# Query projections and one MLP projection of a cross-attention kernel: seven block products in place of eight

## The reference

```python
qh = (q_in @ wq + bq).reshape(b, q_len, H, K)      # H = 16 heads, K = 128
kh = (kv_in @ wk + bk).reshape(b, t, H, K)
vh = (kv_in @ wv + bv).reshape(b, t, H, K)
...
logits = jnp.einsum('bqhk,bthk->bhqt', qh, kh) / scale
weights = jax.nn.softmax(logits, axis=-1)
ctx = jnp.einsum('bhqt,bthk->bqhk', weights, vh).reshape(b, q_len, H * K)
return ctx @ wo + bo
...
h = jax.nn.gelu(h @ w_fc1 + b_fc1, approximate=False) @ w_fc2 + b_fc2   # 512 -> 2048 -> 512
```

## Time and profile before

| | us |
|---|---|
| median of 3 runs (lowest, highest) | 2988.18 (2986.56, 2992.95) |
| the profiled execution, its own time | 2985.3 |
| span in its profile | 2983.5 |
| mean granted TensorE clock | 0.978 of full speed |

### The profile page before, as it was taken

How to read it: one execution, slowest core, us unless ns; L and a number is a source line. 1 busy time by engine, 2 the same in 40 slices (tenths; PEclk the granted TensorE clock), 3 DMA queues, 4 the chain that set the end, 5 groups by cost and what they waited for, 6 DMA issues and landing times.

```text
span 2983.5 us, 40485 instructions
## 1 busy us (share of the span) xinstructions
PE 2823.4 (95%) x14352; PEld 2118.4 (71%) x14352; DVE 1902.5 (64%) x2743; ACT 1099.0 (37%) x2409; POOL 535.6 (18%) x373
## 2 busy tenths in 40 slices
PE   5989898997989999999999999999999999999899
PEld 2333333333778888888888878788888888888687
DVE  5989989897866555556555474565555655555644
ACT  3232323322534333334333343343343433433432
POOL 2857657473001000000000010010000000000100
PEclk8999899998999999999999999999999999999999
DMA  4010010111143222222222211132222222222111
GB/s 164 1 30 29 16 42 0 58 43 43 61 155 124 82 72 94 80 92 82 82 87 77 96 67 63 43 113 81 98 81 82 84 75 98 81 84 75 53 49 56
DMA packets 140224, 215.64 MB, mean 72 GB/s; under 512 B 10033, under 2 KB 76593, under 8 KB 139025
## 3 DMA queue, kind: packets, MB, share of 16 engines
q1 hardware_dynamic: 137264, 210.70, 20.3%
q0 software_dynamic: 2880, 3.94, 0.7%
HBM read 164.53 MB, written 46.14 MB: 71 GB/s over the span
## 4 chain that ended last, share of the span: by engine, by line
PE 64%; DVE 4%; DMA 1%; ACT 1%; issue 1%; DVEq 0%; ACTq 0%; SPq 0%
PE ca_ps L60 19%; PE ca_ps L62 19%; PE ca_ps L61 19%; PE ca_ps L1991 4%; PE ca_ps L1981 4%; DVE ca_stats L68 1%; DMA xres<-pb_dram 1%; PE ca_ps L2018 1%; DVE ca_pb L1745 1%; DMA pb_dram<-ca_pb 0%; ACT ca_pr L1552 0%; DVE ca_pr L1741 0%; DVE ca_mx L1733 0%; DVE ca_ctx_lo L1786 0%; DVE raw L1755 0%
## 5 line engine op out<-in xcount | busy, mean ns | idle before, releaser
L1552 ACT ACTIVATE ca_pr<-ca_ps,ca_nb 128x129 f32<-128x129 f32 x512 | 181.8, 368 | 487.8 <-DVE ca_nb L1735 487.7
L60 PE MATMUL ca_ps<-ca_h_hi,ca_wq_hi 128*128 128x512 f32 x768 | 313.2, 408 | 4.4 <-DVE ca_h_lo L1780 3.9
L617 DVE TENSOR_TENSOR_SCAN tm_xn<-tm_wd,tm_vb 128x512 f32<-128x512 f32 x256 | 298.5, 1208 | 12.7
L1505 POOL TENSOR_TENSOR ca_dv<-ca_bvr 128x256 f32<-128x256 f32 x32 | 23.6, 739 | 1563.7 <-DVE xq L1720 1404.5
L62 PE MATMUL ca_ps<-ca_h_hi,ca_wq_lo 128*128 128x512 f32 x768 | 302.8, 394 | 0.0
L61 PE MATMUL ca_ps<-ca_h_lo,ca_wq_hi 128*128 128x512 f32 x768 | 301.6, 393 | 0.0
L60 PE MATMUL ca_ps<-ca_wv_hi,ca_ctx_hi 128*128 128x256 f32 x1024 | 296.2, 289 | 2.1 <-DVE ca_wv_lo L1715 2.1
L62 PE MATMUL ca_ps<-ca_wv_hi,ca_ctx_lo 128*128 128x256 f32 x1024 | 286.7, 280 | 0.0
L61 PE MATMUL ca_ps<-ca_wv_lo,ca_ctx_hi 128*128 128x256 f32 x1024 | 286.6, 280 | 0.0
L60 PE MATMUL ca_ps<-ca_wo_hi,ca_ct_hi 128*128 128x512 f32 x640 | 256.0, 400 | 1.0 <-DVE ca_ct_lo L1749 0.8
L61 PE MATMUL ca_ps<-ca_wo_lo,ca_ct_hi 128*128 128x512 f32 x640 | 252.7, 395 | 0.0
(11 more groups left out here) (232 smaller groups left out, 5966.5 us busy)
## 6 DMA issues: line engine op xcount, KB each, us to landing
pb_dram<-ca_pb SPq DMA_DIRECT2D x128, 256.0 KB, 2.0
xres<-pb_dram SPq DMA_DIRECT2D x128, 256.0 KB, 2.7
ca_sq<-in_wq SPq DMA_DIRECT2D x49, 512.0 KB, 5.9
ca_so<-in_wo SPq DMA_DIRECT2D x48, 512.0 KB, 3.8
ca_sk<-in_wk SPq DMA_DIRECT2D x33, 512.0 KB, 6.9
ca_sv<-in_wv SPq DMA_DIRECT2D x32, 512.0 KB, 4.0
x_dram<-xres SPq DMA_DIRECT2D x8, 1024.0 KB, 4.2
ca_bvr<-in_bvb SPq DMA_DIRECT2D x32, 256.0 KB, 5.3
```

Of the source, the lines that this page charges most:

```text
L60: pe.matmul(out, lhs[0], rhs[0], start=first, stop=False)
L617: v.tensor_tensor_scan(state[t % 2][:, d, :], wd[:, g].rearrange("p b t -> p (b t)"), pair[:, d, :], 0.0, ALU.mult, ALU.add).then_inc(scan ...
L1552: ins = act.activation(pr[hd][:, b, :], ps[:, BANK_SC + b // 2, o:o + KW], ACT.Exp, bias=nbs[hd][:, b:b + 1], scale=SCALE, accum_out=sms[h ...
```

## The change

In all slots of the attention stages (the first two units of a stage stay as they are) and in the 14 `mlp_slot`s of the second half, the two query projections of a unit (24 matmuls of 512 columns) become `fast`: the product of a 512 x 256 weight block with 512 rows is cut into 2 x 2 blocks and made by Strassen's seven block products, each 2 chunks x 3 matmuls of 256 columns, so 42 matmuls of 256 columns. The products 1 and 6 share bank 0 and the products 2 and 7 share bank 2 (bank 1 in the MLP).

Sums of weight blocks (four for each pair of heads) and of row blocks (four for each quad and stage) are made by POOL, with their `hi` parts by ACT and `lo` parts by DVE (those of the rows by POOL). DVE combines the seven products into the four quarters of the two queries. Sums are also written in place over parts of `wq` and `h` that the plain units have finished with. To make room, `pr` and `pb` (probabilities and transposed blocks) have one buffer in place of two, the output bias is loaded for one stage at a time, and the context of the second half is loaded later (its buffer holds row sums of the first half). Several semaphores are merged. The last pair of a stage is taken out of the loop.

```diff
@@ tensor block @@
+            def fast(C, banks):
+                pe.wait_ge(wq_split, C.wq * 2 + 2)
+                pe.wait_ge(ws_split, C.ws * 2 + 2)
+                pe.wait_ge(t_split, (C.stage * 2 + C.quad) * 3 + 3)
...
+                product(out[0], a11, b11).then_inc(fast_full, 1)
+                product(out[1], s2, t2).then_inc(fast_full, 1)
+                product(out[2], s3, t3).then_inc(fast_full, 1)
+                product(out[3], s1, t1).then_inc(fast_full, 1)
+                product(out[4], a12, b21).then_inc(fast_full, 1)
+                pe.wait_ge(p1_read, C.fast + 1)
+                product(out[0], a22, minus_t4).then_inc(fast_full, 1)
+                pe.wait_ge(fast_sum, C.sums + 1)
+                product(out[1], s4, b22).then_inc(fast_full, 1)
...
             def scores(A, hd):
-                pe.wait_ge(q_out, A.n * 2 + (hd + 1))
+                pe.wait_ge(q_out, A.n * 2 + 2)
...
             def slot(A, C):
                 scores(A, 0)
-                query(C, 0, BANK_Q)
                 key(C, 0)
                 scores(A, 1)
-                query(C, 1, BANK_Q)
+                pe.wait_ge(o_out, A.o * 4)
+                fast(C, Q_BANKS)
                 key(C, 1)
-                value(C, 0, A.o * 4 - 1)
+                pe.wait_ge(q_out, C.n * 2 + 2)
+                value(C, 0, A.o * 4)
                 context(A, 0)
...
             def mlp_slot(B, M, C):
-                for k in range(2):
-                    pe.wait_ge(gelu_ready, M.m * 2 + (k - 3))
-                    hidden(M, k)
+                if M.h == 1:
+                    pe.wait_ge(gelu_step, M.m * 4 - 1)
+                    fast(M, M_BANKS)
...
                 mlp_out(B)
@@ vector block @@
             def slot(A, C):
                 row_max(A, 0)
                 normalise(A, 0)
+                key_col(C, 0)
                 row_max(A, 1)
+                fast_last_quarter(C)
+                normalise(A, 1)
                 if C.quad == 0:
-                    key_col(C, 0)
                     split_one(wv, sv, wv_hi, wv_split, C.wkv)
                 else:
                     split_one(wo, so, wo_hi, wo_split, C.wq)
-                normalise(A, 1)
+                fast_other_quarters(C)
                 if C.quad == 1:
                     split_q(C.wq + 1, 0)
-                else:
-                    key_col(C, 1)
-                if C.quad == 1:
-                    split_q(C.wq + 1, 1)
+                    if more_sums(C):
+                        split_q_fast(C.wq + 1)
+                    else:
+                        split_q(C.wq + 1, 1)
+                key_col(C, 1)
+                if C.quad == 1 and more_sums(C):
+                    weight_sums_lo(N)
+                    weight_sum_in_place_lo(N)
+                value_out(C, 0)
                 context_lo(A, 0)
-                value_out(C, 0)
...
+            def mlp_slot_fast(B, M):
+                if M.quad == 1:
+                    split_one(wo, so, wo_hi, wo_split, M.wq)
+                hidden_quarters(M)
...
+                add_output(B, 0)
+                gelu_lo(M, 0)
+                gelu_lo(M, 1)
+                add_output(B, 1)
+                add_output(B, 2)
+                if M.quad == 1 and more_sums(M):
+                    weight_sums_lo(N)
+                    weight_sum_in_place_lo(N)
+                add_output(B, 3)
@@ scalar block @@
             def second(A, C):
...
                 query_out(C, 1, BANK_K)
-                split_q(C.wq + 1, 1)
+                split_q_fast(C.wq + 1)
+                weight_sum_in_place_hi(N)
+                row_in_place_hi(C)
@@ gpsimd block, after the first pair of a stage @@
+                for g in range(1, G):
+                    if g < G - 1:
+                        gp.wait_ge(fast_full, 7 * unit(g, 1).fast + 7)
+                        weight_sums(unit(g + 1, 0))
+                        weight_sum_in_place()
+                    if g < len(biases):
+                        value_bias(biases[g])
```

More of the change, by code:

```diff
@@ L1294, in cross_attend @@
     TB = 32
+    HALF = QT // 2
+    Q_BANKS, M_BANKS = (0, 2, 3, 4, 7), (0, 1, 5, 4, 7)
     LN_BANKS = (0, 1, 5, 6)
@@ L1372, in __init__ @@
                 self.ln = (h * 3 + st) * 2 + quad
+                self.stage = h * 2 + st
+                self.fast = g * 2 + (quad - 2 + 14 * self.stage)
+                self.sums = self.fast * 5
+                self.plain = 4 * self.stage + 2 * quad + 32 * h
+                self.ws = g + (7 * self.stage - 1)
         class MlpUnit:
@@ L1384, in __init__, with more_sums, sums_before @@
                 self.u = cT if quad else uT
+                self.stage = 4
+                self.fast = g * 2 + (quad - 2 + 14 * self.stage)
+                self.sums = self.fast * 7 - 112
+                self.plain = self.m * 2 + (8 + 8 * h)
+                self.ws = g + (7 * self.stage - 1)
         def units(engine, h, st, slot):
-            with engine.Fori(1, G) as g:
+            with engine.Fori(1, G - 1) as g:
                 slot(Unit(h, st, g - 1, 1), Unit(h, st, g, 0))
                 slot(Unit(h, st, g, 0), Unit(h, st, g, 1))
+            slot(Unit(h, st, G - 2, 1), Unit(h, st, G - 1, 0))
+            slot(Unit(h, st, G - 1, 0), Unit(h, st, G - 1, 1))
+        def more_sums(C):
+            return not isinstance(C.g, int)
+        def sums_before(ln):
+            return 4 * (ln if ln < 4 else max(4, ln - 2))
         def mlp_units(engine, h, slot):
@@ L1462, in _ @@
                     more = h == 0 or i < 15
-                    if h == 0 and i == 1:
-                        for quad in range(2):
-                            sp.wait_ge(c_split, quad + 1)
-                            ctx_in(1, quad)
+                    if i % 8 == 1:
+                        next_bo(h, i // 8)
                     if i > 0:
@@ L1474, in _ @@
                     sp.wait_ge(wq_split, (q + 1) * 2)
+                    sums_taken(h, i)
                     sp.dma_start(sq[:], io["wq"][i + 1]).then_inc(wq_in, 16)
@@ L1480, in _ @@
                     sp.dma_start(so[:], io["wo"][i + 1]).then_inc(wo_in, 16)
+                    if h == 0 and i == 15:
+                        sp.wait_ge(fast_full, 7 * 28)
+                        for quad in range(2):
+                            ctx_in(1, quad)
                 probs(h, 15, 1)
@@ L1486, in _ @@
                     q = h * 24 + i
+                    if i == 17 and h == 0:
+                        next_bo(h, 2)
                     if h == 0 and i == 18:
@@ L1527, in _ @@
+            value_bias(0)
+            stage(0, 0, range(1, 9))
+            stage(0, 1, range(9, 17))
+            add_bo(0, 2, 0)
+            add_bo(0, 2, 1)
+            stage(1, 0, range(17, 25))
+            stage(1, 1, range(25, 32))
+            stage(1, 2, ())
         @block.scalar
@@ new lines, in quarter, with fast_last_quarter @@
+            def quarter(C, hd, out, bank, u):
+                return v.scalar_tensor_tensor(out=out, in0=ps[:, bank, 0:HALF], scalar=head_col(C, "bq", hd), in1=u, op0=ALU.add, op1=ALU.add)
+            def fast_last_quarter(C):
+                v.wait_ge(q_out, C.n * 2)
+                fast_u(C, qT[0][:, 0:HALF], Q_BANKS)
+                quarter(C, 1, qT[1][:, HALF:QT], Q_BANKS[3], u3[:]).then_inc(fast_sum, 1)
+                v.tensor_tensor(x1[:], x1[:], ps[:, Q_BANKS[3], 0:HALF], ALU.add).then_inc(fast_sum, 1)
```

353 lines of the change are left out of this document (290 added, 63 removed).

## The result

The changed kernel takes **3082.04 us** (median of 4 runs, 3071.42 to 3087.90) against 2987.55 of the kernel before: a ratio of 1.031, 95% interval 1.028 to 1.034. The forecast was 3016 within 2980 to 3046: the right sign, and three times too small. The profiled execution took 3071.42 (span 3069.6 against 2983.5).

What follows compares the result with a forecast made beforehand. PE, busy 95% of the span, was taken as the bound. The terms 0 + 7 + 3 + 8 + 3.5 + 4 + 4 = 29.5 on the profiled 2985.3 gave 3014.8; forecast 3016 us, range 2980 to 3046.

Steps and rivals of the forecast that it cites:

- PE's 0.70: Attention slots: PE alone gains about 0.70 us each from the seven products, from 12.89 to 12.19 before the value matmuls.
- PE stays the bound: Rival: DVE's line behind product 4 is shorter by 0.7 or more, each attention slot gains 0.70, 2976 us; chance 0.13.
- near zero: Rival: DVE's line is shorter by about 0.5 a slot, giving 2988 us; chance 0.07.
- 0 for 56 slots: Attention slots: PE's gain becomes an equal wait for DVE's second query, so slots do not get shorter; +-0.3 a slot.
- +7 us: 24 attention slots of quad 1: POOL's weight sums hold DVE's `lo` part, 0.3 a meeting; bounds 0 and 26.
- Weight loads set the pace: Rival: `fast` cannot hide its 42 weight loads, so attention and MLP slots get longer, 3180 us; chance 0.02.
- Joints between steps: Stage joints: scores wait for both queries, +3 at four passing steps; late exponentials, +8 at four first slots.
- Row sums of a stage lie in POOL's idle time: Five stages: row sums fit POOL's idle time but meet DVE's `lo` parts in `second`, +3 us.
- In the MLP's first `fast` ... +3.5: MLP's first `fast`: PE waits for weight sums that can only start after the last plain projection, +3.5 us.
- MLP slots +4: Seven pairs of MLP slots: block 3 waits for DVE's addition of block 1, +4 us; bounds -7 and +12.

Runs made afterwards that it cites:

- run 6: Changed kernel with the splits of the value and output weights moved to the head of the slot on ACT and DVE: 3035.41 us.
- run 11: run 9 with its new one-element tile allocated last, so that the other tiles lie as in run 8: 2975.12 us, ratio 0.9966 to the kernel before.
- run 8: Changed kernel with a plain last MLP, the slots of run 6 and the joints' work rearranged on POOL, DVE, ACT and PE: 2983.87 us.
- run 7: Changed kernel with DVE adding the MLP's second output block ahead of the `lo` part of the second Gelu: 3068.44 us.
- run 1: Changed kernel with the plain `mlp_slot` and its sums put back for half 1, attention left as changed: 3044.93 us.
- run 3: Changed kernel with ACT reading the passing step's two queries ahead of the `hi` parts of weight and row sums: 3088.71 us.
- run 4: Changed kernel with the first quad's row sums split earlier, their `hi` parts ahead of head 1's exponentials: 3078.95 us.
- run 2: Changed kernel with POOL's output bias of the second quad and first value bias moved behind the first pair's sums: 3062.02 us.
- run 9: run 8 with the in-place weight sum split in the first slot and a one-element exponential on ACT ahead of the queries: 2983.45 us.
- run 12: run 9 once more, on the same chip as run 11: 2983.19 us.

## Why the prediction was right and wrong

**Right: where the slots' gain went.** The text said that PE's 0.70 turns into a wait for DVE of the same size. A wait of that size did come, in all 56 slots (0.65 to 0.93 between two starts instead of 0.23), with the value products mostly at 12.97 and 13.06 for a forecast of 12.9. The prices that I took on a line between rows came out as taken: 0.42 and 0.48 for 256 elements. DVE was released 0.2 to 0.3 later than forecast, and its line from there was 0.1 to 0.2 shorter. Run 6 shows the cause from the other side. The rivals "PE stays the bound" and "near zero" are out.

**In part luck: the size.** The 52 steady slots cost 10.9 where the steps "0 for 56 slots" and "+7 us" gave 7, but the 7 had another reason. No run shows the 0.3 for each meeting with POOL, my estimate, in which DVE waits for the rest of POOL's operation: DVE's `lo` part took 1.18 or 1.19 in slots with POOL's sums beside it and in slots without; it was POOL's sum that took 1.66 in place of 0.74. What the slots lost is this: PE alone would need 25.33 (run 6) and not 25.86, the wait takes 0.6, and the 24 value products behind the wait take 0.13 more than without it. The two slots of a stage that stand outside the loop lost 0.02 and 0.07, the eleven inside it 0.24 on the mean; why DVE is released later in those is open.

**Nearly right: the products.** `fast` takes 5.04 and not 4.91, since its 256-column matmuls are spaced 0.118 and not 0.1146, and the scores of head 1 ahead of it take 0.88 and not 0.81; the key projections take 2.88 and 2.76, as forecast (means over the 52 slots of run 11). So PE alone stands at 25.33, as runs 6, 8 and 11 have it, not 25.2: the gain in the steady slots is 0.52 each, not 0.70. The ratio 0.118 to 0.230 (2.76 for 12 key products) is a half. The rival "Weight loads set the pace", which needed a spacing over 0.13, is out as well.

**Wrong: the step "Joints between steps", with "Row sums of a stage lie in POOL's idle time".** Together they had 14 us (3 for the passing joints, 8 for the first slots, 3 for the row sums); measured: 22.2 + 14.6 + 3.4 + 1.4 = 41.6. I priced each new operation where it would be needed and took POOL to be free to begin there ("POOL's two in-place sums begin after PE has ended the query"). It was not: its own line runs from 931.01 to 959.9 without 1 us of pause. I never added up that line. From rows that I had, it is easily done: four row sums of 512 elements at up to 1.46 (5.8), four of 256 at 0.74 (3.0), the biases' 5.85 and 0.74, and the `lo` parts of two quads, 2048 elements each (11.7 at the same price): about 27 us, in a step of 30. Three things follow, none of which I had. PE's scores stand 3.7 us, because ACT's `hi` parts of the row sums stand ahead of the queries (I let ACT be at the queries at once). After the pause PE runs at a granted clock of 0.50. And the exponentials of the first slot begin 959.96 - 954.23 = 5.7 us after its scores, where I had 4.4: the in-place sums come last in POOL's line. No single run takes POOL's line away alone, so how the 41.6 divide between these is not shown. Runs 3 and 4 show that ACT's order by itself does not free the joints, and run 8, which takes the `lo` parts off POOL and turns the order round on three engines, brings the seconds and first slots from 263.0 to 248.0 against 226.2 before.

**Wrong, by the same omission: "In the MLP's first `fast` ... +3.5".** It is about 21: the MLP's part of 32.8 less 10.4 that run 7 gave back and 1.5 that run 1 kept. I counted the splits behind the last projection and not POOL's line ahead of it, which again is busy from 2864.34 to 2889, nor that these splits are slower beside it. The clock adds to it: 24 matmuls at a granted clock of 0.50, spaced 0.213 instead of 0.118, are 2.3.

**Mis-sized: "MLP slots +4".** It was 10.4, within the bounds of -7 to +12 (a pair of units took 23.84 in place of 22.30). The mechanism was the one named (block 3 waits for DVE's addition, the group of waits on L2016); run 7 removed most of it.

So the slots gave 4 more than forecast, the joints 28, the MLP's start 17, its slots 6: 55 of the 86.1 - 29.5 = 56.6 that the sum lacked against the profiled execution. The median lies 8 further up.

**The layer norm's 4.92** was not in the sum either; run 4 gives no price for it, since the time did not fall when it went. I had read in the earlier trace rows that an operation with two inputs in SBUF meets POOL, and looked for such operations only. The four here have one input of 512 elements, and they met POOL too: 4.92 with POOL's `lo` parts beside them (from 931.01), 1.92 in run 4, where POOL stood still at that time (932.89 to 935.04).

**Open.** The first slots of run 11 are still 1.7 above those of the kernel before, and three of its four seconds 1.9 to 2.9; no run tells what of this is POOL and what PE's clock. Whether a shorter POOL line alone (fewer elements) would free the joints was not tried. Whether other places of the weights make PE's slots shorter still was not tried either.

## What to carry to other kernels

Add up the whole line of the engine that gets the new work, from its last free moment to the first consumer, before you price one operation of it; a low share of busy time over the kernel (POOL 18%) says nothing about one step of 30 us. When a faster engine turns into a waiting one, look on the slower engine for a piece of work ahead of the awaited result that could fill one of its own pauses: here one such move was worth 38 us, and in the kernel without the change nothing. Work that happens once per stage is where an algebraic saving in the loop can be lost, and joints want one rearrangement of all their queues: here single moves passed most of the wait on. And when executions of one kernel lie 16 us apart, compare the part that was edited and not the total.

## What the runs showed of the hardware

- Beside POOL's sums, DVE's operations on one SBUF input of 512 elements took 4.92 us for four (930.15) in place of 1.92 (run 4), one with two inputs in SBUF up to 2.25 in place of 0.68 (run 2), and one with 4 elements 0.57 in place of 0.17 (run 9, 952.10). Those with an input in PSUM kept 0.67 to 0.69. It can go the other way: in the steady slots DVE's `lo` part kept its 1.18, and POOL's sum, begun 0.1 after it, took 1.66 in place of 0.74.
- After a pause of 3.7 us PE's granted clock was 0.50 for about 5 us; after 16.7 us it was 0.50 for about the first 5 us of products. After a pause of 3.68 us in run 6 it fell to 0.50 only 1.2 us after PE had begun again, and once more behind the next pause, of 2.78 us.
- With a small shift in the place of operands the same matmuls took another time: the second key projection of a slot from 2.76 to 2.79 us, the 24 value products behind it from 2.74 to 2.84, while the first key projection kept 2.88; worth 8 us in this kernel (runs 11 and 12).
- A load of ACT's table took 1.28 us in every place where it stood (a mean of 1283 ns in each group of the kernel before, of the changed one and of runs 8, 9 and 11); one dummy exponential in ACT's idle time ahead of it took it off the path (with one split moved, 2.5 us in three of the four first slots, 1.0 in the fourth; run 9).
